# Set-up with graph 0's rows ahead of the attention columns, and a tail with products ahead of transposes, tables in pieces and the register loaded among products

## The reference

```python
xn = layernorm(x)                                  # 128 graphs x 128 nodes x 256
Xw = xn @ Wv + bv
e  = leaky_relu((Xw @ aw[:d])[:, None, :] + (Xw @ aw[d:])[:, :, None] + ab)
A  = adj * exp(e);  T = A / (A.sum(-1) + 1e-12)
H  = xn @ Wk[0] + bk[0] + T @ xn @ Wk[1] + bk[1] + T @ T @ xn @ Wk[2] + bk[2]
x  = x + relu(H)

f = layernorm(x)                                   # 16384 tokens x 256
p = softmax(f @ switch_w.T + switch_b)             # 16 experts
e = argmax(p); pos = place of the token in its expert's queue, in token order
y = f @ expert_w[e].T + expert_b[e] if pos < 1228 else f
x = x + y * max(p)
```

## Time and profile before

| | us |
|---|---|
| median of 3 runs | 768.35 (768.01 to 769.15) |
| the profiled execution | 767.28 |
| its span, first to last instruction | 765.5 |
| TensorE busy | 711.6 (93%) |
| VectorE busy | 647.9 (85%) |
| ScalarE busy | 480.2 (63%) |
| GpSimd busy | 444.1 (58%) |
| mean granted TensorE clock | 0.985 |

### The profile page before, as it was taken

One profiled execution on the slowest core, in us unless ns is written; L12 is line 12 of the kernel. 1 busy time (PEld: TensorE's weight loads), 2 busy tenths in 40 slices (PEclk: granted clock), 3 DMA queues, 4 the chain that ended last, 5 costly groups with the idle time before them and its releaser, 6 DMA issues.

```text
span 765.5 us, 18802 instructions
## 1 busy us (share of the span) xinstructions
PE 711.6 (93%) x4791; PEld 624.2 (82%) x4791; DVE 647.9 (85%) x3100; ACT 480.2 (63%) x1504; POOL 444.1 (58%) x523
## 2 busy tenths in 40 slices
PE   1899999999999999999999999999999999877783
PEld 1788888778888888898889899898889899756663
DVE  3799999999989999899989999999989988785552
ACT  1457777766666666666666666666666766654551
POOL 4224445546666666666656666666666665575563
PEclk9999999999999999999999999999999999979998
DMA  9423444433344444444443344444443323353430
GB/s 266 118 85 97 138 138 154 151 127 119 123 144 153 147 146 153 128 150 139 146 141 118 121 143 149 145 140 147 134 134 128 115 89 101 99 167 112 120 104 1
DMA packets 93035, 100.15 MB, mean 131 GB/s; under 512 B 10427, under 2 KB 85240, under 8 KB 92930
## 3 DMA queue, kind: packets, MB, share of 16 engines
q1 hardware_dynamic: 77860, 66.74, 30.1%
q0 software_dynamic: 13008, 30.07, 10.8%
q10 hardware_dynamic: 2064, 2.13, 1.1%
HBM read 49.92 MB, written 54.72 MB: 137 GB/s over the span
## 4 chain that ended last, share of the span: by engine, by line
PE 86%; DVE 6%; issue 3%; ACT 1%; SPq 1%; DMA 1%; POOL 1%; POOLq 0%; DVEq 0%; ACTq 0%
PE ps_z12a L1160 11%; PE ps_z12b L1160 11%; PE ps_lgb L1160 9%; PE ps_z0a L1160 9%; PE ps_z0b L1160 8%; PE ps_lga L1254 6%; PE ps_z0b L1261 4%; PE ps_z0a L1261 4%; PE ps_z12b L1220 4%; PE ps_xt L1194 3%; PE ps_xt L1188 3%; PE ps_z12a L1220 3%; PE ps_lgb L1290 3%; PE ps_t L1242 2%; PE ps_t L1211 2%
## 5 line engine op out<-in xcount | busy, mean ns | idle before, releaser
L524 POOL DMA_INDIRECT out<-lent,tok x143 | 145.8, 1020 | 151.3 <-DVE lent L1121 136.0
L507 POOL DMA_INDIRECT rowbuf<-rows,idx x128 | 129.8, 1014 | 55.0 <-issue 30.1
L572 ACT CAST xth<-ps_xt 128x256 fp32r<-128x256 f32 x128 | 47.8, 373 | 123.6 <-PE ps_xt L1194 123.3
L475 POOL TENSOR_SCALAR x<-xin,nm,r 128x256 f32<-128x256 f32 x128 | 85.1, 665 | 27.6 <-PE ps_xt L1194 19.3
L1254 PEld LDWEIGHTS ps_lga<-swc,xft 128*128 128x128 f32 x512 | 76.8, 191 | 14.2 <-ACT xft L575 3.4
L646 ACT ACTIVATE x<-rin 128x256 f32<-128x256 f32 x143 | 86.8, 608 | 1.7 <-DMA rin<-rowbuf 1.7
L471 POOL TENSOR_TENSOR r<-ve,mhalf 128x4 f32<-128x4 f32 x32 | 34.2, 1069 | 77.7 <-ACT ve L618 77.7
L588 ACT ACTIVATE od<-rows,oc,oa 128x256 f32<-128x256 f32 x128 | 77.0, 602 | 0.1
L753 DVE TENSOR_TENSOR xtl<-ps_xt,xth 128x256 fp32r<-128x256 f32 x128 | 54.0, 422 | 20.6 <-ACT xft L575 19.6
L1254 PE MATMUL ps_lga<-swc,xft 128*128 128x16 f32 x512 | 66.2, 243 | 2.9 <-ACT xft L575 2.9
L1194 PE MATMUL ps_xt<-ident,x 128*128 128x128 f32 x256 | 49.5, 275 | 9.4 <-POOL x L475 8.5
(11 more groups left out here) (205 smaller groups left out, 2358.8 us busy)
## 6 DMA issues: line engine op xcount, KB each, us to landing
rin<-rowbuf SPq DMA_DIRECT2D x143, 130.0 KB, 2.3
xin<-in_x SPq DMA_DIRECT2D x32, 512.0 KB, 4.0
out<-od SPq DMA_DIRECT2D x32, 512.0 KB, 5.4
ain<-in_adj SPq DMA_DIRECT2D x32, 256.0 KB, 4.6
ewr<-in_ewT SPq DMA_DIRECT2D x16, 256.0 KB, 2.9
out<-lent,tok POOLq DMA_INDIRECT x143, 3.0
rowbuf<-rin ACTq DMA_DIRECT2D x1, 2080.0 KB, 10.8
rowbuf<-rows,idx POOLq DMA_INDIRECT x128
```

The costliest lines, as they stand in the source:

```text
L475: pool.tensor_scalar(x0[:, g % 2, :], xin[:, g % BODY, :], nm1[:, q, g % G:g % G + 1], r1[:, q, g % G:g % G + 1], ALU.add, ALU.mult).then_ ...
L507: pool.indirect_dma_start(out=rowbuf, out_offset=bass.IndirectOffsetOnAxis(ap=idx[:, i:i + 1], axis=0), in_=rows[:, r, :], in_offset=None, ...
L524: pool.indirect_dma_start(out=out.rearrange("g n d -> (g n) d"), out_offset=bass.IndirectOffsetOnAxis(ap=tok[:, i % RY:i % RY + 1], axis=0 ...
```

## The change

Set-up: Wk[2] and Wk[1] are issued by ScalarE at its start, with a semaphore of their own, and Wk[0] behind an early exponential; the biases and the router's weights also get their own semaphores and go behind the inputs. ScalarE does graph 0's nm and ve before it splits w12, in two halves. VectorE does four graphs' moments, then the set-up's broadcasts and w12l, then xtl of graph 0, then the attention columns, then the moments of graphs 4 to 6; the hop biases are added at the end of slot 0. TensorE's products for cvec come after graph 0's transposes. GpSimd does one power early (first), and zeroes ebp in slots 4 and 5 and not at the start; the load of the expert biases moves behind c = 1 of SyncE's loop.

Tail: TensorE's tile(i) is expert(i), then turn(i+2); the expert number of tile i+1 is loaded behind the second product of tile i. ScalarE's is high(i+1) and norm(i+2), VectorE's low(i+1) and finish(i). last_step and last_tiles are cut into three and six pieces, one behind each of the tiles 99 to 107.

```diff
@@ block.sync
-            sp.dma_start(bkr, ...).then_inc(d_w, 16)
-            for kt in range(KT):
-                ks = slice(kt * P, (kt + 1) * P)
-                sp.dma_start(w12r[:, kt, 0:D], Wk[2, ks, :]).then_inc(d_w, 16)
-                sp.dma_start(w12r[:, kt, D:2 * D], Wk[1, ks, :]).then_inc(d_w, 16)
-                sp.dma_start(w0r[:, kt, 0:D], Wk[0, ks, :]).then_inc(d_w, 16)
             sp.dma_start(xin[:, G:2 * G, :], xd[1]).then_inc(d_x[1], 16)
             sp.dma_start(ain[:, 0:G, :], ad[0]).then_inc(d_a[0], 16)
...
+            sp.dma_start(bkr, ...).then_inc(d_bk, 16)
@@ block.gpsimd
+                if it * BODY + k in (4, 5):
+                    half = (it * BODY + k - 4) * E * D // 2
+                    pool.memset(ebp[:, half:half + E * D // 2].bitcast(F32), 0.0).then_inc(s_ebz, 1)
+            pool.tensor_tensor(first[:], onesf[:, 0:G], mhalf[:], ALU.pow)
@@ block.scalar
-            act.wait_ge(s_fill, 1)
-            act.wait_ge(d_w, 16 * (3 * KT + 3))
-            act.copy(w12h[:], w12r).then_inc(s_wh, 1)
+            w12d = [Wk[2].rearrange("(t p) d -> p t d", p=P), Wk[1].rearrange("(t p) d -> p t d", p=P)]
+            for h in range(2):
+                act.dma_start(w12r[:, :, h * D:(h + 1) * D], w12d[h]).then_inc(d_w12, 16)
+            act.wait_ge(s_pc, 2)
+            act.activation(e1[:, 0, 0:1], onesf[:, 0:1], ACT.Exp)
+            act.dma_start(w0r[:, :, 0:D], Wk[0].rearrange("(t p) d -> p t d", p=P)).then_inc(d_w0, 16)
...
             def tile(i):
+                if i + 1 < NT:
+                    high(i + 1)
                 if i + 2 < NT:
-                    high(i + 2)
-                if i + 3 < NT:
-                    norm(i + 3)
+                    norm(i + 2)
-            phase_a(act, slot_fn, -LEAD_STATS, LAG_OUT)
+            for k in range(-LEAD_STATS, G - LEAD_STATS + 1):
+                slot_fn(0, k)
+            act.wait_ge(d_w12, 32)
+            for kt in range(KT):
+                act.copy(w12h[:, kt, :], w12r[:, kt, :]).then_inc(s_wh, 1)
+            phase_a(act, slot_fn, G - LEAD_STATS + 1, LAG_OUT)
@@ block.vector
             def tile(i):
-                if i + 2 < NT:
-                    low(i + 2)
+                if i + 1 < NT:
+                    low(i + 1)
                 finish(i)
+                turn = i - (WOVEN + LAG_ROUTE + 1 - REST - G)
+                if 0 <= turn < 3:
+                    last_step(NG - 1, turn)
+                if 3 <= turn < 9:
+                    last_tiles(turn - 3)
...
             dve.wait_ge(s_pc, 12)
+            for k in range(-LEAD_STATS, -LEAD_STATS + G + 1):
+                slot_fn(0, k)
             dve.wait_ge(d_v, 16 * 4)
             for t in range(KT):
                 link(dve.tensor_scalar(bvb[:, t, :], onesf[:], bvt[:, t:t + 1], None, ALU.mult))
-            for k in range(-LEAD_STATS, -LEAD_STATS + G + 1):
+            remainders()
+            for k in range(-LEAD_STATS + G + 1, 0):
                 slot_fn(0, k)
-            set_up()
-            phase_a(dve, slot_fn, -LEAD_STATS + G + 1, LAG_OUT)
+            attention_columns()
+            for g in range(G, LEAD_STATS):
+                input_stats(0, g)
+                if g < LEAD_STATS - 1:
+                    input_moments(0, g)
+            slot_fn(0, 0)
+            hop_biases()
+            phase_a(dve, slot_fn, 1, LAG_OUT)
@@ block.tensor
+            def expert_of(i):
+                pe.wait_ge(s_tab, step_of(i))
+                e = pe.value_load(tab_exp[0:1, i:i + 1], min_val=0, max_val=E - 1)
+                at[i] = [pe.snap(e * EW + t * D) for t in range(KT)], pe.snap(e * D)
...
+                    if ahead is not None and (part, t) == (0, 1):
+                        expert_of(ahead)
...
             def tile(i):
+                expert(i, i + 1 if i + 1 < NT else None)
                 if i + 2 < NT:
                     turn(i + 2)
-                expert(i)
```

More of the change, by code:

```diff
@@ L103, in graph_then_experts @@
         abt = sb("abt", [P, 1])
+        first = sb("first", [P, G])
         cvec = sb("cvec", [P, NV])
@@ L427, in _ @@
                     load_expert(2 * c + 4)
+                if c == 1:
+                    load_biases()
                 if 2 <= c < NG + 2:
@@ L673, in link, with remainders, attention_columns @@
                 dve.wait_ge(s_vc, vc[0])
[L675 to L679, removed]
-                dve.wait_ge(s_wh, 1)
-                link(dve.tensor_tensor(w12l[:], w12r, w12h[:].bitcast(F32), ALU.subtract))
+            def remainders():
+                for kt in range(KT):
+                    dve.wait_ge(s_wh, kt + 1)
+                    dve.tensor_tensor(w12l[:, kt, :], w12r[:, kt, :], w12h[:, kt, :].bitcast(F32),
+                                      ALU.subtract).then_inc(s_w12l, 1)
+            def attention_columns():
+                dve.wait_ge(d_w0, 16)
                 dve.wait_ge(s_pe0, 1)
@@ L813, in slot_fn @@
                 g = k + LEAD_STATS
-                if valid(it, g):
-                    if g % G == 0:
-                        dve.wait_ge(d_x[g % BODY // G], 16 * it + 16 * (g // BODY) + 16)
-                    dve.bn_stats(st1[:, g % 2, :], xin[:, g % BODY, :]).then_inc(s_st1, 1)
+                if valid(it, g) and not G <= it * BODY + g < LEAD_STATS:
+                    input_stats(it, g)
                 if counts is not None:
@@ L860, in slot_fn @@
                 if s == B + REST:
-                    for i in range(2):
-                        low(WOVEN + i)
+                    low(WOVEN)
                 i = tailed(it, k)
@@ new lines, in last_tiles @@
+                if turn == 3:
+                    link(10, dve.tensor_reduce(base[:], pick, AX_X, ALU.add))
+                    link(11, dve.tensor_tensor(kept[:, 0:E], count, most[:], ALU.min))
+                    link(12, dve.tensor_tensor(fall[:], kept[:, 0:E], kept[:, 1:1 + E], ALU.subtract))
+                if turn == 4:
+                    link(13, dve.tensor_tensor(pick, past, by_expert(fall[:], LASTS), ALU.mult))
+                    link(14, dve.tensor_reduce(stop[:], pick, AX_X, ALU.add))
@@ L1151, in _ @@
                               start=(t == 0), stop=(t == KT - 1))
-            for t in range(KT):
-                mm = pe.matmul(ps_set[:, 2 * KT:2 * KT + 2], bvb[:, t, :], awt[:, :, t],
-                               start=(t == 0), stop=(t == KT - 1))
-            mm.then_inc(s_pe0, 1)
             def product(psum_out, part, lhs_h, lhs_l, rhs_h, rhs_l, start=False, stop=False):
@@ L1307, in expert @@
                     ts = slice(t * P, (t + 1) * P)
-                    w = bass.ds(e * EW + t * D, D)
-                    product(y, part, xth[:, c, ts], xtl[:, c, ts], ewh_f[:, w], ewl_f[:, w],
-                            start=(part == 0 and t == 0))
-                pe.matmul(y, two_ones[:], ebp[:, bass.ds(e * D, D)], start=False, stop=True,
+                    product(y, part, xth[:, c, ts], xtl[:, c, ts], ewh_f[:, bass.ds(w[t], D)],
+                            ewl_f[:, bass.ds(w[t], D)], start=(part == 0 and t == 0))
+                    if ahead is not None and (part, t) == (0, 1):
+                        expert_of(ahead)
+                pe.matmul(y, two_ones[:], ebp[:, bass.ds(bias, D)], start=False, stop=True,
                           skip_group_check=True).then_inc(b_y, 1)
             def tile(i):
+                expert(i, i + 1 if i + 1 < NT else None)
                 if i + 2 < NT:
                     turn(i + 2)
-                expert(i)
-            phase_a(pe, slot_fn, -LEAD_XT, LAG_OUT)
+            slot_fn(0, -LEAD_XT)
+            pe.wait_ge(s_vc, KT)
+            for t in range(KT):
+                mm = pe.matmul(ps_set[:, 2 * KT:2 * KT + 2], bvb[:, t, :], awt[:, :, t],
+                               start=(t == 0), stop=(t == KT - 1))
+            mm.then_inc(s_pe0, 1)
+            phase_a(pe, slot_fn, 0, LAG_OUT)
             for i in range(WOVEN + LAG_OUT - REST - 1, NT):
```

165 lines of the change are left out of this document (95 added, 70 removed).

## The result

The changed kernel took 762.63 us (median of 4 runs, 762.37 to 763.86), the kernel before 768.43 beside it: ratio 0.9927, 95% interval 0.991 to 0.9944. That is 5.8 less; 11.0 less was forecast, 757.4, and 762.63 lies just above the range of 752 to 762. The profiled execution took 763.86, its span is 762.1 (before 765.5).

A forecast was written before the change was run, and what follows sets the result against it. TensorE bounds the middle, so only the two ends were priced: start 6.8 plus tail 4.1 gives 10.9 off the profiled 767.28, 756.4; the median of runs lies 1.07 above, so 757.4, range 752 to 762.

The forecast's parts named there:

- Start: Set-up up to svs of slot 0: svs from 24.48 to 17.3, less 0.4 for hop biases, gain 6.8 us.
- Landing: Set-up: graph 0's input, issued first beside weight transfers, lands between 4.8 and 6.2; 5.5 taken.
- The upper end of 7.9: Set-up: largest gain allowed for the start, 7.9 us, if graph 0's input lands at 4.8.
- Tail, the load: Tail tiles: moving the register load behind the second product changes nothing, bounds -0.1 to +0.2 us per tile.
- Rival C: Tail: queued products cover the register load, tile falls to 1.43, 7 us less, 750.5 in all; chance 0.11.
- Tail, products ahead of transposes: Tail: tile 102's product no longer waits for tile 104's row tile; the 1.48 us wait goes.
- Tail, tables in pieces: Tiles 99 to 107: 9.4 us of table work spread in pieces; ten tiles 18.8, 2.4 over 16.3.
- The 20.7 given as the sign: Tail: sign of being right, tile 109's product some 20.7 us after tile 99's, against 24.75 before.
- the row tile of tile 108: Tail: next wait after the pieces; tile 108's transposes at 692.5, tile 109 at 696.1 instead of 700.50.
- the wait of 4.49 behind the chain: Tail: 4.49 us behind VectorE's chain for the last tables, counted among 8.4 lost in ten tiles.
- Rival B: Start or tail gives little, through a transfer, half clock, VectorE's pieces or the row tile; typical 761; chance 0.27.
- the 0.97: Set-up: GpSimd's first power took 2.01, median 1.04; an early one makes the counted one 0.97 us shorter.

The follow-up runs named there:

- load_only: Kernel before with the new set-up; in the tail only the register load moved behind the second product of the tile before; 761.64 us, ratio 0.9902.
- again: The changed kernel run once more without any change, in a session without late signals; 758.07 us, ratio 0.9862 to the kernel before.
- start_only: Changed kernel with its new set-up, but the tail as in the kernel before; 760.73 us, ratio 0.9907, in a session without late signals.
- before2: The kernel before, run again unchanged with its own profile in a session with late signals; 767.67 us, ratio 1.0.
- pieces_only: Kernel before with the new set-up; in the tail only the tables are cut into pieces, old order, load ahead of its product; 763.96 us, ratio 0.994.

## Why the prediction was wrong

**Start: right in its steps, with errors that cancel.** Landing 5.5 forecast, 5.74 measured (4.9 after issue beside ScalarE's transfers, 4.0 alone); the power 8.5 and short, 8.99 and 1.01 long; transposes 10.8 and 11.54, of which 0.35 is the first x (1.27 in the chain, before 0.92) and the rest stands ahead of the power; xtl's end 12.4 and 13.1; the columns' end 15.0 and 15.3; svs 17.3 and 17.30, behind three graphs' moments as said. That svs agrees to the hundredth is luck: everything ahead of it was 0.2 to 0.7 late, and the last stretch took 2.0 and not 2.24. Gain 6.8 forecast; 6.8 and 7.4 by the medians of the start alone, 6.88 at graph 127 in this profile, but 6.4 to 9.3 there over the changed kernel's six. The upper end of 7.9 was added up without the 0.4 for the hop biases; it should be 7.5.

**Tail, the load: right in size.** No gain and no loss a tile was forecast, bounds -0.1 to +0.2; periods of the two places overlap (1.61 to 1.65 with the load ahead, 1.60 to 1.66 behind the second product, tiles 112 to 142). Its place gave 1.8 once, which the sum has not, and load_only did not repeat it late. Rival C's loop was forecast at 1.43 and measured at 1.46 with load and address arithmetic gone, but the changed kernel does not get there: the two products ahead do not cover the load.

**Tail, products ahead of transposes: the 1.48 went,** since in again no transpose before tile 108's waits for a row tile by more than 0.21. Tile 99 starts 17.4 after svs of graph 127 and not 18.8, a gain of 1.4 that the sum has not. It goes with the new order: 17.2 to 18.0 in all undisturbed profiles that have it, start_only 18.4.

**Tail, tables in pieces: the step that failed.** Of 8.4 lost in ten tiles 4.4 were to be won, less 0.26 behind them. The 20.7 given as the sign is 24.75 less 4.1; by the sum's own 4.4 it is 20.35. Two things are wrong in it. First, undisturbed the ten tiles took 23.5 and 24.2. The tiles of the pieces took 2.1 and not 1.9, which is hidden by the row tile of tile 108. Its transposes start at 686.86 in again; 692.5 less the start's 6.35 there is 686.15, so that step was 0.7 short. I added nothing for the clock behind it, and the two tiles from 687.17 to 691.45 took 4.28 and not 3.3: another 1.0. The stretch of again between them:

```profile
686.80:690.20 3.40, 3.22 (x14) 2.98 (x15) 1.07 (x5) 1.13 (x3) 0.91 (x1) 0.50 0.42 125
```

Tile 109 was forecast at 689.75 in that frame and came at 691.45. With the 1.4 won ahead of tile 99 included, the tail of again gave 2.6 of 4.1 (94.79 against 97.43). So the undisturbed 758.07 and 757.35 stand near the forecast of 757.4 partly by luck: the gains were 9.5 and 10.1, not 11.0, beside a kernel before that was 0.8 and 0.9 faster than the one that the forecast starts from.

Second, and this is what moved the time out of the range: the wait of 4.49 behind the chain was taken as pure loss. In four of six groups TensorE's signals come late there, by about 2.5 and 5. Kernels with whole tables hide this in that wait: ahead of tile 104 they take 34.4 to 35.2 undisturbed and 34.6 to 36.0 late. With pieces the 27.0 to 28.5 become 33.6 to 35.1. The sum had no term for a signal that arrives after its product's record. In the first measurement against again, tile 99 to 100 takes 1.8 more, 103 to 104 4.9 more, 104 to 109 1.8 less (the clock at half for 13.6, but no separate wait for tile 108's row tile), 100 to 103 0.1 less: together the 4.8 between 28.30 and 23.47. Rival B, one end gives little, typical 761, is what the time looks like, by a mechanism that it did not name: what was late first was not a piece or the row tile, but a signal from an engine that by its own record was done. I looked only for what is late next in a trace that had no such signal.

**Left open.** What makes the signals late. It is not the change (before2 has them), not the chip, not one order of the tail, and they stand around the same tiles, 98 to 100 and 102 to 105, in the late profiles. Whether the register loads or the last stores are needed for them was not seen, since both trials ran undisturbed. The recording of the profile itself may be part of it, since SyncE's odd issue times come with it; no run excludes it. The Trainium skill, "NOTIFIC — the notification-queue block", section 7.1 on overflow, says that the block which writes an engine's records can hold the engine back when its inner queues fill. That would fit signals that are late in every kernel of a session; no run here shows it.

## What to carry to other kernels

Before a wait is priced as loss, ask what else ends inside it: an engine that waits for one thing hides every later arrival of the others, and a trace of one execution shows only those that it happened to have. When a gain on paper is a few us in 760, measure both kernels in more than one session: here the same two programs were 5.5 and 10.1 apart. Work that is spread in pieces between tiles is not free where TensorE is at half clock: after the stop at 679.7 the granted clock was 0.50 for 13.6 us, through four tiles of 2.4 to 2.6 each, and a tile without a piece took 1.94 at that clock. And the last piece ends later than the whole chain would (693.7 against 681.8 in two late profiles), so ask who waits for its result: in pieces_only that was a stop of 2.3.

## What the runs showed of the hardware that was not expected

- TensorE's signal can reach other engines 2.4 to 5.2 us after the record of the matmul that sends it, and in some sessions does so at the same place in every kernel tried, the unchanged one included.
- A matmul's record is no proof that its result is there: engines that waited for it alone started 5 us behind it.
- A register load on TensorE with its address arithmetic costs a tile 0.17 (1.63 against 1.46) even where two products are queued ahead of it; the pause in the record is 0.33 at either place.
- GpSimd's first power took 2.01 in the kernel before. With one made early on ones, none of the 32 that count took over 1.04. But the early one, which is now the first, took 1.04 itself, so the 0.97 is not shown to be the price of being first; what it was for stays open.

```profile
L539 POOL TENSOR_TENSOR first<-onesf,mhalf x1: 1040/1040/1040, 3.0 to 3.0; 128x4 f32<-128x4 f32 x1
...
L477 POOL TENSOR_TENSOR r<-ve,mhalf x32: 1007/1040/1040, 9.0 to 621.5; 128x4 f32<-128x4 f32 x32
```
